# A Mamba-style scan layer on eight cores: the product of step and x goes to GpSimd, and the output chain on VectorE is laid over two slots

## The reference, cut to what matters

```python
xn = layernorm(x)                                   # [16, 2048, 1024]
x_and_res = xn @ in_proj_w.T + in_proj_b
x_in, res = silu(x_and_res[..., :1024]), x_and_res[..., 1024:]
ssm = x_in @ x_proj_w.T + x_proj_b                  # 16 columns for the step, then B, then C
delta = clip(softplus(ssm[..., :16] @ dt_proj_w.T + dt_proj_b), 1e-5, 0.1)
A = clip(-exp(A_log), -5.0, -0.01)                  # [1024, 16]
h = clip(h * exp(A * dt) + (Bt * dt * xt), -100, 100)   # for each time step; 16 states for each channel
y = sum(h over the 16 states) * Ct + D_param * xt
out = x + (y * silu(res)) @ out_proj_w.T + out_proj_b + ffn(xn)   # ffn(xn) is one matrix of 1024 by 1024
```

## Time and profile before

| what | value |
|---|---|
| time, median of 3 runs | 1353.47 us (1353.25 to 1353.56) |
| profiled execution, its own time | 1354.87 us |
| its span on the slowest core (core 3) | 1353.3 us |
| span of the fastest core | 1349.8 us |
| busy: DVE, ACT, PE, POOL | 98%, 89%, 79%, 5% |
| mean granted PE clock, core 3 | 0.906 |

### The profile page before, as it was taken

The page is one execution under the profiler, slowest core; times in us unless marked ns, Lnnn a source line. Parts: engine busy times, 40 slices in busy tenths (PEclk is TensorE's granted clock), DMA queues, the critical chain, the costliest instruction groups (busy, mean ns, idle before and its releaser), DMA issues.

```text
span 1353.3 us, 16308 instructions; the slowest of 8 cores (1349.8 to 1353.3 us)
## 1 busy us (share of the span) xinstructions
PE 1066.4 (79%) x4392; PEld 433.5 (32%) x4392; DVE 1321.3 (98%) x688; ACT 1198.9 (89%) x1924; POOL 72.6 (5%) x101
## 2 busy tenths in 40 slices
PE   6686777789778888878877886878877887887876
PEld 3232332233223333333323332333323332333332
DVE  6899998999999999999999999999999999999997
ACT  3899997999899999999999998999988888888872
POOL 1001100000000000000000000000000000011000
PEclk9888988899899988889889898889979999988899
DMA  9657688555555556545555645554554446466443
GB/s 284 97 112 138 140 137 190 118 111 139 142 121 140 117 129 155 139 105 136 128 149 122 142 124 130 148 119 111 136 145 90 109 108 138 102 142 142 118 94 70
DMA packets 126249, 176.45 MB, mean 130 GB/s; under 512 B 31232, under 2 KB 87104, under 8 KB 126160
## 3 DMA queue, kind: packets, MB, share of 16 engines
q1 hardware_dynamic: 112480, 150.49, 41.8%
q0 software_dynamic: 13680, 24.91, 15.2%
HBM read 101.45 MB, written 35.65 MB: 101 GB/s over the span
## 4 chain that ended last, share of the span: by engine, by line
DVE 39%; issue 32%; PE 16%; DMA 7%; ACT 4%; DVEq 1%; SPq 0%; ACTq 0%
DVE h L753 32%; PE pS L513 9%; DMA u<-u 6%; DVE pS L772 2%; ACT da L928 2%; PE pB L479 1%; PE pX L445 1%; PE pO L445 1%; DVE u L803 1%; DMA xnT<-xn 1%; DVE carry L736 1%; PE pC L489 1%; DVE pS L779 1%; PE pR L499 1%; DVE u L784 1%
## 5 line engine op out<-in xcount | busy, mean ns | idle before, releaser
L753 DVE TENSOR_TENSOR_SCAN h<-da,u 128x4112 f16<-128x4112 f16 (+1 forms) x134 | 1110.4, 8327 | 6.5 <-ACT da L928 5.7
L928 ACT ACTIVATE da<-dl,consb 128x512 f16<-128x512 f16 x1024 | 640.2, 709 | 1.5 <-DVE dl L775 0.7
L513 PE MATMUL pS<-h,eye 128*128 128x512 f16 x1024 | 314.7, 461 | 244.0 <-DVE h L753 244.0
L513 PEld LDWEIGHTS pS<-h,eye 128*128 128x128 f16 x1024 | 105.8, 111 | 430.4 <-issue 366.5
L479 PE MATMUL pB<-xin,wx 128*128 128x512 f16 x512 | 137.0, 416 | 0.6 <-DVE Bf L795 0.6
L499 PE MATMUL pR<-xnT,win 128*128 128x512 f16 x512 | 125.6, 390 | 0.0
L489 PE MATMUL pC<-xin,wx 128*128 128x512 f16 x512 | 122.0, 382 | 0.0
L375 POOL DMA_DIRECT2D yt<-ost x56 | 47.9, 865 | 1066.0 <-ACT ost L989 992.4
L445 PE MATMUL pX<-xnT,win 128*128 128x512 f16 x352 | 85.0, 386 | 7.4 <-DMA xnT<-xn 5.4
L965 ACT ACT_TABLE_LOAD x64 | 82.1, 1283 | 5.7 <-PE pR L499 4.6
L928 ACT ACT_TABLE_LOAD x63 | 80.8, 1283 | 1.3
(11 more groups left out here) (146 smaller groups left out, 889.5 us busy)
## 6 DMA issues: line engine op xcount, KB each, us to landing
u<-u SPq DMA_DIRECT2D x62, 896.0 KB, 5.6
wo<-wos SPq DMA_DIRECT2D x56, 512.0 KB, 7.3
xtile<-x SPq DMA_DIRECT2D x48, 512.0 KB, 6.4
yt<-xt SPq DMA_DIRECT2D x56, 256.0 KB, 7.6
yt<-ost POOLq DMA_DIRECT2D x56, 256.0 KB, 5.2
wx<-w_x POOLq DMA_DIRECT2D x15, 256.0 KB, 6.7
xnT<-x SPq DMA_DIRECT2D x4, 512.0 KB, 7.0
da<-w_in SPq DMA_DIRECT2D x4, 512.0 KB, 11.3
```

The lines of the kernel that those rows point to most:

```text
L513: mm = te.matmul(pS[s % 2][:, :], eye[:, :], h[:, n * SEG + 2:(n + 1) * SEG], start=(n == 0), stop=(n == NST - 1))
L753: v.tensor_tensor_scan(h[:, n0 * SEG:n1 * SEG], da[:, n0 * SEG:n1 * SEG], u[p][:, 0:(n1 - n0) * SEG], 0.0, op0=ALU.mult, op1=ALU.add).then ...
L928: sc.activation(da[:, n * SEG + 2:(n + 1) * SEG], dl[s % 2][:, :], AF.Exp, scale=cc(C_AL + k * NST + n)).then_inc(act_da, 1)
```

## The change

On DVE the product of step and x leaves the slots 1 to 62 (for the tiles w = 2 to 63) and becomes `step_x` on POOL, which starts once scan A of the slot is done. The step's clip moves to the front of its slot, ahead of scan A. The output chain of a tile is spread over two slots: times C and add D of tile s-1 stay in slot s, times R of tile s-2 comes in slot s, right behind scan A. Both `clip_carry` instructions now stand between times C and add D. On ACT the gate's Silu is a slot later. On PE the product for C comes ahead of the sums of scan A (unless two x tiles are due), that for R behind the one for B, and the output tiles are a slot later, as are their loads and evacuations; the products of the last chunk's outputs are cut at other places.

```diff
@@ schedule
-            out_at[b + DCH + q] += [(c - 1, m) for m in ms]
+            late = 0 if c == NCH - 1 or (c == NCH - 2 and q == DCH - 1) else 1
+            out_at[b + DCH + q + late] += [(c - 1, m) for m in ms]
@@ gpsimd
+            def step_x(w):
+                c, k = divmod(w, DCH)
+                gp.wait_ge(v_cl, w + 1)
+                gp.wait_ge(v_scan, scans(w - 1, groups(w - 1)[0][1]))
+                gp.tensor_mul(t1[w % 2], dl[w % 2][:, :], seg(xin[c % 2], k)).then_inc(g_t1, 1)
             for s in range(0, NSL):
+                if 1 <= s < NSL - 1:
+                    step_x(s + 1)
                 for (c, m) in out_at[s - 1]:
                     accumulate(c, m)
@@ tensor, within a slot
-                if 0 <= s < NSL:
+                if few:
                     R_mm(s)
                 ...
-                if 0 <= s < NSL:
-                    sums(s, 1 if few else 0)
-                    if not few:
-                        if s + 2 < NSL:
-                            dt_mm(s + 2)
-                            B_mm(s + 2)
+                if few:
+                    sums(s, 1)
+                elif 2 <= s < NSL:
+                    if len(xin_at[s]) < 2:
+                        C_mm(s)
+                    sums(s, 0)
+                    if s + 2 < NSL:
+                        dt_mm(s + 2)
+                        B_mm(s + 2)
+                    R_mm(s)
+                    if len(xin_at[s]) == 2:
                         C_mm(s)
@@ vector, within a slot (z = s - 1, w = s + 1)
+                if 2 <= w < NSL:
+                    clip_step(w)
                 if 0 <= s < NSL:
                     scan(s, *groups(s)[0])
-                if 0 <= s - 1 and keeps(s - 1):
-                    clip_carry(s - 1, 8)
+                if 2 <= s < NSL:
+                    times_R(s - 2)
+                if z >= 0:
+                    times_C(z)
+                if z >= 0 and keeps(z):
+                    clip_carry(z, 8)
+                if 0 <= s < NSL and keeps(s) and not few:
+                    clip_carry(s, 0)
+                if z >= 0:
+                    add_D(z)
+                ...
+                elif w < NSL:
+                    v.wait_ge(g_t1, w - 1)
+                    v.wait_ge(act_B, w)
+                    v.tensor_mul(u[w % 2][:, 2:SEG], Bf[w % 2][:, :], t1[w % 2]).then_inc(v_u, 1)
@@ scalar
             def silus(s):
-                silu_R(s)
+                if s >= 1:
+                    silu_R(s - 1)
+                if s == NSL - 1:
+                    silu_R(s)
```

More of the change, by code:

```diff
@@ L755, in scan, with clip_step, times_C, add_D @@
                                      0.0, op0=ALU.mult, op1=ALU.add).then_inc(v_scan, 1)
+            def clip_step(w):
+                v.wait_ge(act_ln, w + 1)
+                v.tensor_scalar(dl[w % 2][:, :], dl[w % 2][:, :], 0.1, 1e-5,
+                                op0=ALU.min, op1=ALU.max).then_inc(v_cl, 1)
+            def times_C(z):
+                v.wait_ge(pe_s, scans(z))
+                v.wait_ge(act_C, z + 1)
+                v.tensor_mul(pS[z % 2][:, :], pS[z % 2][:, :], Cf[z % 2][:, :]).then_inc(v_SC, 1)
+            def add_D(z):
+                c, k = divmod(z, DCH)
+                v.wait_ge(v_SC, z + 1)
+                v.scalar_tensor_tensor(pS[z % 2][:, :], seg(xin[c % 2], k), cc(C_D + k), pS[z % 2][:, :],
+                                       op0=ALU.mult, op1=ALU.add).then_inc(v_D, 1)
+            def times_R(z):
+                c, k = divmod(z, DCH)
+                v.wait_ge(v_D, z + 1)
+                v.wait_ge(act_R, z + 1)
+                if c >= 2 and k == 0:
+                    v.wait_ge(pe_o, (c - 1) * DCH)
+                if c == 1 and k == 0:
+                    v.wait_ge(d_wff, 32)
+                v.tensor_mul(seg(yb[c % 2], k), pS[z % 2][:, :], rs[z % 2][:, :]).then_inc(v_y, 1)
             for s in range(-1, NSL + 1):
+                z, w = s - 1, s + 1
+                if 2 <= w < NSL:
+                    clip_step(w)
                 if 0 <= s < NSL:
                     scan(s, *groups(s)[0])
-                if 0 <= s - 1 and keeps(s - 1):
-                    clip_carry(s - 1, 8)
                 if s == 0:
@@ L766, in _ @@
                     evac_xT(1, 1)
[L767 to L782, removed]
-                    v.wait_ge(v_cl, w + 1)
[L784 to L792, removed]
@@ L793, in _ @@
-                if w == 0:
-                    v.wait_ge(pe_B, 1)
-                    v.tensor_scalar(Bf[0][:, :], pB[:, :], cc(C_BB), None, op0=ALU.add).then_inc(v_B0, 1)
-                if w < NSL:
+                few = 0 <= s < NSL and len(groups(s)) == 4
+                if 2 <= s < NSL:
[6 more added lines that the diff above has]
+                    clip_carry(s, 0)
@@ L797, in _ @@
+                if z >= 0:
+                    add_D(z)
+                if w < 2:
+                    clip_step(w)
+                    if w == 0:
+                        v.wait_ge(pe_B, 1)
+                        v.tensor_scalar(Bf[0][:, :], pB[:, :], cc(C_BB), None, op0=ALU.add).then_inc(v_B0, 1)
+                    v.wait_ge(v_cl, w + 1)
+                    v.tensor_mul(t1[w], dl[w][:, :], seg(xin[0], w)).then_inc(v_t1, 1)
                     v.wait_ge(v_t1, w + 1)
@@ L812, in _ @@
                 if 0 <= s < NSL:
-                    few = len(groups(s)) == 4
-                    if keeps(s) and not few:
-                        clip_carry(s, 0)
                     for g in groups(s)[1:-1]:
                         scan(s, *g)
+                        if s == NSL - 1 and g == groups(s)[1]:
+                            times_R(s - 1)
                     if keeps(s) and few:
```

29 lines of the change are left out of this document (14 added, 15 removed).

## The result

The changed kernel takes 1362.09 us in the median of 6 runs (1358.34 to 1363.47), the kernel before 1353.59 beside it on the same chip. The ratio is 1.0056, with a 95% interval of 1.0041 to 1.0071: slower by half a per cent, where 1348.4 was predicted.

What follows compares the result with a forecast made beforehand. DVE was taken to set the pace in nearly every slot: 16.8 us saved there, less 0.8 in the first nine slots and 10.9 for held clips, leaves 5.1, so 1353.47 goes to 1348.4 us, range 1336 to 1358.

Steps and rivals of the forecast that it cites:

- DVE's chain: On DVE, shorter start-to-start distances save 0.30, 0.23 or 0.16 us a slot by number of carry clips, 16.8 in all.
- POOL's product: Step times x on POOL takes 1.17 us, starts 0.25 after scan A and ends 1.42 after it.
- Held clips: On DVE the carry clips wait for POOL's product, delaying add D by 0.27 us a slot, 10.9 in all; chance 0.40.
- nothing held: Rival: POOL's product does not delay DVE's carry clips, so all 16.0 us stay saved: 1337.5 us; chance 0.32.
- The likeliest case: Carry clips on DVE fully held until POOL's product ends, leaving 5.1 us saved: 1348.4 us; chance 0.40.
- The first nine slots: ACT is later there; without slot 0's Silu it gains 3.2 us, slot 9's scan starts 2.1 earlier, 0.8 is lost.
- The accumulating DMA goes out up to 2 us later; its buffer is wanted again two tiles later: nothing: In POOL's queue the accumulating DMA stands behind step times x, at no cost.
- no loss, the worst copy aside: The copy of u still lands in time for scan A; only the worst copy costs some tenths of a us, as before.
- Output tiles a slot later move the same work: Moving the output tiles one slot later shifts the same work, with no cost put on it.
- POOL late, slower than before: Rival: POOL starts 0.60 us after the scan, ends at 1.77, and held clips delay add D by 0.62: 1363; chance 0.18.
- ACT in front of the step's clip: Rival: ACT's Ln comes late for the step's clip, 0.3 us in 18 slots, 5 us: 1353, no change; chance 0.10.

Runs made afterwards that it cites:

- the two one-sided experiments: The kernel with both edits but step times x back on DVE, 1357.55 us; the kernel before with only that product moved to POOL, 1358.33 us.
- both edits: The changed kernel with R of slot 1 moved to the front of slot 2 on PE and POOL's DMAs issued ahead of its product: 1345.22 us, ratio 0.9921.
- the product-alone kernel: The kernel before with only step times x of slots 1 to 62 moved to POOL, POOL's DMAs staying ahead of it: 1358.33 us, ratio 1.003.

## Why the prediction was wrong, step by step

Forecast were 1348.4 us, with a range of 1336 to 1358; measured were 1362.09. The sum for DVE's own chain held. What failed are two terms outside it: POOL's DMAs behind the product, put at nothing, cost 12.6 us of waits on the slowest core, and the Silu that leaves slot 0, put down as a gain for ACT, cost 7.8. Moving either back takes its wait away.

- **DVE's chain, 0.30, 0.23 and 0.16 a slot, and 16.8 in all:** right. Measured 0.27 and 0.14, about 15.1 in all. The basis was right as well: the row of times C to add D (0.78) priced the new order, and the two one-sided experiments show that it is the dependent pairs, not the busy time, that decide.
- **POOL's product 1.17 us, 0.25 after scan A:** nearly right, 1.144 us and 0.17. The end is at 1.31 us in place of 1.42. By the prediction's own rows two streams come to 0.10 + 1.02 = 1.12, a little under the "1.14 to 1.17" that it wrote. The estimate from the Trainium skill's "GPSIMD Engine Reference", section "3.1 Elementwise — side-by-side cycle accounting" (1.17), was 0.03 too high.
- **Held clips, 0.27 a slot and 10.9 us:** the mechanism is right, as the clips moved forward show (0.81 a slot), the term was mis-sized. With an end at 1.31 add D starts at 1.34 after the scan instead of 1.56; against the 1.29 of a slot with nothing held that leaves 0.05. The slip is a tenth of a microsecond in POOL's end, and another tenth in that I let the clips begin only after it and take their whole length from there, while add D in fact starts 0.03 behind POOL's end. The likeliest case was thus wrong by some 9 us, to the side of "nothing held".
- **The first nine slots, "0.8 goes":** one of the two steps that failed most. It counted the Silu that leaves slot 0 as 3.2 us won for ACT and did not ask who waits for that Silu. R of slot 1 does, on a single bank, and all of slot 1's sums but the first four stand behind R on PE: 7.84 us. And the 3.2 us were not to be had in slot 9 on the slowest core. With slot 2 repaired (both edits, core 1) PE starts the x tiles of chunk 2 at 218.97 and ACT their `xin` at 222.75, which is where they stood before (219.35 and 222.88): a transposing DMA paces them, not ACT's list. Ln then starts at 233.23 (before 233.37), and the clip at 233.93 waits 6.95 us where I had put the scan at 231.0.
- **"The accumulating DMA goes out up to 2 us later; its buffer is wanted again two tiles later: nothing":** wrong. I looked at the buffer that the DMA frees and not at what it runs beside. Issued before the end of scan A it is out of the way of the copy of `u`; issued behind the product it runs beside it: 12.6 us in seven slots on core 7, 8.0 in the mean over the cores, more than slot 2. With it went the "no loss, the worst copy aside". The experiment moved the accumulating and the residual DMAs together, so which of them does it is not told apart. The two long waits on core 7 stand where three DMAs (two of them accumulating, slot 57) and four (all residual, slot 58) leave POOL behind one product; behind one or two the wait is 1.5 us at most.
- **"Output tiles a slot later move the same work":** wrong at the end, but small. Two outputs come into slot 55, beside one of the last chunk's products, and with the copies repaired times C of slot 56 waits 0.5 to 3.2 us for sums. The last sums cost 0.35 us more at a granted clock of 1.00, and 2.3 more at 0.81. Where the 0.35 come from is open: the kernel before with the product on POOL has them too (1.70).
- **The rivals:** none was the one that came. The time fell on that of "POOL late, slower than before" (1363), but not by its mechanism: POOL was early. That the time was close to that rival is chance. "ACT in front of the step's clip" did not cost in regular slots, and the four waits for Ln that the core shows lie in slots up to 9.

What stays open: why the mean granted clock was 0.79 to 0.82 on all cores in the first result and 0.85 to 0.91 in the same kernel on another chip; how much of the first ratio (1.0056 against 1.0033 there) comes from it beyond the 2 us at the tail; and what makes six slots of the product-alone kernel 0.3 us longer: the idle time lies ahead of the product by B, of add D or of scan A or B, in most with nothing in the trace that releases it.

## What to carry to other kernels

When an instruction moves a slot later on one engine, write down which buffer it frees, who writes that buffer next, and what stands behind that writer in its queue; do it for the ends of the loop apart, since a slot with slack in the middle has none there. A compute instruction that goes onto a queue that also issues DMAs goes behind them if they are due earlier, or it sends them into the transfer that the next step waits for; where several are due at once it then comes late itself (1.26 us in one slot here). When a wait has several conditions, look up in the kernel which of them it can be: the view named sums that the scan had no need of, and hid 4.9 us of late copy. And price a new order by the distances between dependent instructions in the trace: the product was worth 0.34 us by its row and 0.0 or 0.27 by its neighbours.

## What the runs showed that was not expected

- With transfers of DRAM tiles issued from POOL within 1.3 us of the copy of `u`, the copy's median over the eight cores was 6.1 to 7.4 us in place of 5.2 to 5.6, and its longest 10 to 14; with them issued before scan A's end where they were due, on another chip, the median was 4.9 to 5.3, where the changed kernel had 5.9 to 7.5 on a third. The copy's own bytes and issue were the same.
- DVE starts its next instruction 0.02 to 0.03 us after the end of the product on POOL that held it, against 0.14 to 0.17 us from the end of a scan to POOL's start. In slot 1 a single clip of 8 columns took 0.83 us in the records (70.34, with POOL at 69.99 for 1.16): a held instruction shows as long, not as late.
- A product on POOL that depends on DVE and is waited for by DVE costs the way twice: in the product-alone kernel it starts 0.50 us after the start of the clip that it needs (0.28 long) and the reader starts 0.18 after its end, 1.82 us for 0.20 + 0.34 on DVE's own list.
- From 750 to 770 us of the first result PE was granted 0.81, between its levels of 1.2 GHz (0.50) and 2.4 GHz (1.00), and eight matmuls took 2.27 us in place of 1.89; it had 18.66 of these 20 us busy. Regular slots on DVE did not get longer by it; the last times C did, 3.65 us of waiting at 0.81 against 1.70 at 1.00 with the same list of instructions.
